# Half a step between scores and transposed scores, with the value products moved into the waits

## What is computed

```python
xn = layernorm(x)
x = x + attention0(xn) + ffn0(xn)   # key k is seen by query q where k <= q; softmax over keys
                                    # ffn0: 128 -> 512 -> gelu -> 128, inputs of both products block-quantized
xn = layernorm(x)
x = x + attention1(xn) + moe1(xn)   # causal; exp(sim - max), divided by (sum + 1e-8)
                                    # moe1: sum over 8 experts of (silu(xn @ wg) * (xn @ wu)) @ wd, 128 -> 512 -> 128
```

## Time and profile before

| what | value |
|---|---|
| median of 3 runs | 1661.28 us (1660.81 to 1663.71) |
| the profiled execution | 1662.67 us, span 1661.0 us |
| layer 0 loop, 44 to 710 us | 665.9 us; PE busy 463.6, DVE 322.4, ACT 295.9, POOL 192.1; mean clock 0.66 |
| layer 1 loop, 785 to 1640 us | 855.0 us; PE busy 819.9, DVE 658.4, ACT 507.5, POOL 448.0; mean clock 0.98 |

### The profile page before, as it was taken

One profiled execution on the slowest core, in us unless ns is written; L12 is line 12 of the kernel. 1 busy time (PEld: TensorE's weight loads), 2 busy tenths in 40 slices (PEclk: granted clock), 3 DMA queues, 4 the chain that ended last, 5 costly groups with the idle time before them and its releaser, 6 DMA issues. The chain is left out here.

```text
span 1661.0 us, 22555 instructions
## 1 busy us (share of the span) xinstructions
PE 1349.9 (81%) x7928; PEld 769.6 (46%) x7928; DVE 1032.5 (62%) x2380; ACT 827.6 (50%) x1220; POOL 681.7 (41%) x791
## 2 busy tenths in 40 slices
PE   3577767677776766644999999999999999999987
PEld 1233323333333333322556566665665656666655
DVE  5454545454545444412778787787877878878753
ACT  2444444444444443421656566565665656656650
POOL 3131324241323222332555555555555555655540
PEclk7566667676766666665999999999999999999997
DMA  5212223232222221214110111001111011000003
GB/s 155 61 53 60 60 60 98 60 98 60 81 71 72 69 86 33 67 66 114 37 28 23 47 33 44 28 24 46 34 44 28 24 46 33 25 28 24 15 14 109
DMA packets 49420, 89.67 MB, mean 54 GB/s; under 512 B 7639, under 2 KB 18396, under 8 KB 46238
## 3 DMA queue, kind: packets, MB, share of 16 engines
q1 hardware_dynamic: 48158, 87.72, 17.5%
q10 hardware_dynamic: 1152, 0.52, 0.1%
HBM read 41.69 MB, written 44.31 MB: 52 GB/s over the span
## 5 line engine op out<-in xcount | busy, mean ns | idle before, releaser
L135 PE MATMUL bank_pair<-st 24*128 24x512 f32 (+3 forms) x1024 | 234.4, 449 | 218.2 <-DVE l_mx L662 159.3
L662 DVE TENSOR_REDUCE l_mx<-bank_pair 128x2 f32<-128x1024 f32 (+1 forms) x192 | 200.4, 1045 | 320.7 <-PE bank_pair L900 320.7
L1127 POOL TENSOR_TENSOR a_h_lo<-a_h,a_h_hi 128x512 fp32r<-128x512 f32 x256 | 328.9, 1285 | 165.8 <-ACT a_h_hi L1174 164.2
L135 PEld LDWEIGHTS bank_pair<-st 24*128 24x128 f32 x1024 | 121.3, 223 | 355.9 <-issue 178.8
L1235 DVE SCALAR_TENSOR_TENSOR a_h<-a_h,bank_pair 128x512 f32<-128x512 f32 x256 | 175.4, 685 | 145.0 <-ACT a_h L1170 145.0
L749 ACT ACTIVATE l_E<-bank_pair 128x1024 f32<-128x1024 f32 (+1 forms) x192 | 168.4, 883 | 172.6 <-PE bank_pair L142 172.5
L169 DVE CUSTOM_DVE_ANT_0 bank_pair<-bank_pair,mask 128x512 f32<-128x512 f32 (+3 forms) x512 | 238.1, 517 | 8.3 <-PE bank_pair L135 8.0
L1174 ACT ACTIVATE a_h_hi<-a_h 128x512 fp32r<-128x512 f32 x256 | 161.5, 631 | 133.5 <-DVE a_h L1241 130.6
L1181 ACT ACTIVATE a_E<-bank_pair 128x1024 f32<-128x1024 f32 (+1 forms) x192 | 169.8, 884 | 115.6 <-PE bank_pair L142 115.6
L142 PE MATMUL bank_pair<-st 28*128 28x512 f32 (+3 forms) x1024 | 204.0, 438 | 1.2 <-ACT l_E L749 1.2
L1241 DVE TENSOR_TENSOR a_h<-a_h,bank 128x512 f32<-128x512 f32 x256 | 176.0, 688 | 26.7
(11 more groups left out here) (127 smaller groups left out, 2213.7 us busy)
## 6 DMA issues: line engine op xcount, KB each, us to landing
st<-stack_d SPq DMA_DIRECT2D x128, 192.0 KB
stack_d<-l_q_k_hi SPq DMA_DIRECT2D x64, 256.0 KB
stack_d<-l_q_k_lo SPq DMA_DIRECT2D x32, 256.0 KB
o_d<-l_O SPq DMA_DIRECT2D x32, 256.0 KB, 2.0
o_d<-a_O SPq DMA_DIRECT2D x32, 256.0 KB, 2.0
l_at<-o_d SPq DMA_DIRECT2D x8, 256.0 KB, 3.7
l_share<-rden_d SPq DMA_DIRECT2D x8, 256.0 KB, 3.3
a_wst<-wg_in SPq DMA_DIRECT2D x8, 256.0 KB, 2.7
```

The costliest lines, as they stand in the source:

```text
L135: return nc.tensor.matmul(bank[:, col:col + w], st[rows, j, 0, bass.ts(t, P)], st[rows, j, 1, 0:w], start=first, stop=last)
L662: nc.vector.tensor_reduce(out, src, AX.X, ALU.max).then_inc(S_used, 1)
L1127: nc.gpsimd.tensor_tensor(h_lo[:, q % RH, :], h[:, q % RH, :], h_hi[:, q % RH, :].bitcast(F32), ALU.subtract).then_inc(h_lo_ready, 1)
```

## The change

**Row groups go by heads.** The row group is now 64 r + 32 j: a quad fills all four row groups of its own `st` tile (four tiles in place of two). Its stack comes in four DMAs of 24 rows in place of two, and the maxima in two DMAs of 4 rows x 512 in place of 4 x 2 x 512; the rows that selected the plane are gone.

**Order in layer 0.** S units are cut as T units are: 512, then 384 + 128, then 256 keys, for each plane; so there are eight reductions a quad in place of six. In step g the first three positions carry T of quad g-1, units 3 to 5, and the last three T of quad g, units 0 to 2. PV of quad g-1 stands in step g behind position 4 (its first two key blocks) and behind position 5 (the other two). `turn_input(0, ..)` goes behind position 2, `project_attention` behind position 3. The order on ScalarE, POOL and DVE follows; `magic_tile` goes behind the second reduction, `store_outputs` one step later.

**Gelus.** The fc tiles are written one by one into `pv_bank` and `C_bank`, two at the end of step u == 0, one behind position 0 and one behind position 1 of u == 1; four gelus in place of two. Gelus take no bank pair any more. `keep_warm`, which nothing called, is removed.

**Layer 1.** S units are taken in the order 3, 4, 5, 0, 1, 2 (plane 1 first) so that S and T mostly lie on other row groups; `load_expert` is issued one quad later.

```diff
-def row_of(g, r):
-    return HALF * r + GROUP * (g % STACKS_A_BUFFER)
+def row_of(r, j):
+    return HALF * r + GROUP * j
 ...
-            put(("T", g, n), 0 <= g < QUADS)
+            put(("T", g - 1, n + 3) if n < 3 else ("T", g, n - 3), 0 <= (g - 1 if n < 3 else g) < QUADS)
 ...
                 scores_and_keys(g, 4)
+                if in_range(g - 1):
+                    PV(g - 1, 0)
+                    PV(g - 1, 1)
                 if q is not None:
                     turn_tile(q, min(b + 2 if u >= 2 else b + 1, B))
                 scores_and_keys(g, 5)
+                if in_range(g - 1):
+                    PV(g - 1, 2)
+                    PV(g - 1, 3)
                 if q is not None:
                     proj(q)
...
-                if in_range(g):
-                    for kb in range(NT):
-                        PV(g, kb)
 ...
-            def fc(a, half):
-                begin("F", a, half)
+            def fc(a, t):
+                if t == 0:
+                    pe.wait_ge(xqT_ready, a + 1)
+                    if a == 0:
+                        pe.wait_ge(bias_in, 16)
+                        pe.wait_ge(pv_set, 1)
+                    else:
+                        pe.wait_ge(O_copied, QUADS_A_BATCH * a)
+                elif t == 1:
+                    if a > 0:
+                        pe.wait_ge(y_added, NT * a)
+                else:
+                    pe.wait_ge(gelu_ready, NT * a + t - 1)
+                nc.tensor.matmul(h_bank(t)[:, :], xqT[:, bass.ts(t, P)], wfc[:, :], start=True, stop=False)
+                nc.tensor.matmul(h_bank(t)[:, :], onesb[:, :], bfc[:, :], start=False, stop=True).then_inc(h_ready, 1)
 ...
-                if 2 * g % B == 0 and x < EXPERTS:
+                if 2 * g % B == 2 and x < EXPERTS:
                     sp.wait_ge(w_lo_ready, 3 * x)
                     load_expert(x)
```

More of the change, by code:

```diff
@@ L128, in spread, with scores, keys_by_queries @@
     return nc.tensor.matmul(bank[:, :], sel[rows, b % 2, :], rden[rows, :], start=True, stop=True)
[L131 to L138, removed]
-    kb, col = block
[L141 to L148, removed]
+def scores(nc, bank, st, r, j, block, first, last):
+    kb, col = block
+    t, w, rows = NT - 1 - kb, width(kb), slice(row_of(r, j), row_of(r, j) + SLOT_ROWS)
+    return nc.tensor.matmul(bank[:, col:col + w], st[rows, 0, bass.ts(t, P)], st[rows, 1, 0:w], start=first, stop=last)
+def keys_by_queries(nc, bank, st, r, j, block):
+    kb, col = block
+    w, rows = width(kb), slice(row_of(r, j), row_of(r, j) + ROWS)
+    return nc.tensor.matmul(bank[:, col:col + w], st[rows, 1, bass.ts(kb, P)], st[rows, 0, N - w:N], start=True, stop=True)
 def values_by_probs(nc, pv_bank, V, E, g, kb, slots):
@@ L375, in _ @@
             load_x(1, B, x_rest_in)
[L376 to L380, removed]
+            sp.wait_ge(rows_set, 1)
+            for st in stacks:
+                for part in range(MROWS):
+                    sp.dma_start(st[SLOT_ROWS + part:P:GROUP, 1, :].bitcast(F32), st_rows[:, :]).then_inc(rows_in, 16)
             def bring_bias():
@@ L495, in rest_of_setup @@
                 nc.gpsimd.memset(mask[:, :], 0.0).then_inc(set_up, 1)
[L496 to L501, removed]
-                                            pattern=[[0, N]], channel_multiplier=-1 if plane == 0 else 1).then_inc(rows_set, 1)
+                nc.gpsimd.memset(st_rows[:, :], 1.0).then_inc(rows_set, 1)
                 pool.wait_ge(set_up, 1)
@@ L537, in _ @@
                 if in_range(g):
-                    for n in range(2, UNITS_A_QUAD):
+                    for n in range(3):
                         causal(g, n)
@@ L697, in _ @@
                     maxima_of(g + 1, 0)
-                if q is not None:
-                    magic_tile(q)
                 if u == 0 and ok(b + 1):
@@ L703, in _ @@
                     maxima_of(g + 1, 1)
+                if q is not None:
+                    magic_tile(q)
                 if u == 1 and ok(y2):
@@ L844, in _ @@
                 if in_range(g):
[L845 to L846 removed]
+                    exp(g, 1)
                 if q is not None:
@@ L857, in _ @@
                 if u == 0 and ok(b):
-                    gelus(b, 0)
-                    gelus(b, 1)
+                    for t in range(NT):
+                        gelus(b, t)
                 if g == FIRST + 3:
@@ L870, in scores_and_keys @@
             def scores_and_keys(g, n):
-                more, here = in_range(g + 1), in_range(g)
+                back, m = (g - 1, n + 3) if n < 3 else (g, n - 3)
+                more, here = in_range(g + 1), in_range(back)
                 if more:
```

207 lines of the change are left out of this document (102 added, 105 removed).

## The result

The changed kernel takes 1553.2 us at the median of four runs (1552.5 to 1553.8), against 1662.5 us for the kernel before beside it: a ratio of 0.934, 95% interval 0.932 to 0.936. The forecast was 1605 us. One execution in all the experiments, 1522.5 us of e10, ran in a slower state and is left out of that kernel's median.

A forecast was written before the change was run, and what follows sets the result against it. Layer 0 was taken as bound by a chain of waits, layer 1 by PE's own products. -44 - 11 - 6 + 5 + 0 = -56 us from 1662.67 gave 1606.7, as a median 1605 us; range 1575 to 1660.

The forecast's parts named there:

- The step's end: Layer 0, maxima to next S: S follows at once and the maxima's DMA is hidden, -4.1 us a step.
- PV in two waits: Layer 0, positions 4 and 5: PV's first part sticks out by 1.95 us, its last costs 0.78, +2.7 a step.
- The clock: Layer 0: step's end runs warm (+0.8 gained), next step's position 2 may be cold (0.5 lost), -0.3 us a step.
- Eight reductions: Layer 0, DVE: two more reductions a quad each cost the fixed part of 0.15 us, +0.3 a step.
- Fc and gelus: Two fc tiles moved into waits, -2.16 us; longer gelu chain, +1.3; net -0.8 a batch, -6 us.
- rival 4: Gelu table loads on ScalarE cost an added 1.38 us drain per switch, as the skill page says: 1627 us, chance 0.03.
- project_attention: Layer 0: moved behind position 3 it falls into a wait of 1.41 us, -11 us for 8 batches.
- Input transpose: `turn_input(0, ..)` gives up its place on the path but waits for `normalize` on DVE: nothing either way.
- Loop ends: End of layer 0's loop: the last quad's T is finished a half step later, +5 us, of 3 to 7.
- DMAs: Stack loads: four of 96 KB replace two of 192 KB, issued with PE waiting for nothing they hold; counted as 0.
- Layer 1: Shared row groups of S and T +6 us, later `load_expert` -6: zero, of -7 to +12.
- rival 3: Layer 0: all of PV runs warm, -2.8 us a step, -102 in all: 1559 us, chance 0.12.

The follow-up runs named there:

- e10: Changed kernel with three unread 128x512 matmuls behind positions 1, 2 and 3 of layer 0 steps (2 and 3 only where u == 1): 1507.1 us.
- e5: Changed kernel with T in step with S again (no half step) and four E slots instead of three: 1741.1 us.
- e12: Kernel before the change with three unread 128x512 matmuls behind positions 1, 2 and 3 of every layer 0 step: 1632.6 us.
- e2: Changed kernel with PV's first two key blocks moved behind position 5, so all of PV is one block ahead of the projection: 1605.4 us.
- e1: Changed kernel with all four PV blocks moved behind the maxima rows, at the very end of each step: 1615.2 us.
- e3: Changed kernel with all four fc tiles at the end of the step with u == 0: 1581.1 us.
- e7: Changed kernel with project_attention back at the step's end, ahead of the maxima rows, and add_attention behind the negations: 1555.9 us.
- e8: Changed kernel with normalize behind the third reduction, input transposes behind position 3, tile's magic at the previous step's end (except a batch's first tile): 1536.1 us.
- e9: Kernel before the change with one edit, layer 1's expert loads issued one quad later: 1655.9 us.
- e4: Changed kernel with layer 1's S units in natural order (plane 0 first): 1566.3 us.
- e6: Kernel before the change with each query or key store to the DRAM image in 16 groups of 8 rows instead of 8 of 16: 1652.3 us.

## Why the prediction was half right, step by step

- **The step's end, -4.1.** Right: the gap is 0.33 us. That the wait for the maxima's DMA is hidden was right too; e5 shows it at 3.0 us a step when it isn't. Missed was the second use of the half step, S and T in different rows.
- **PV in two waits, +2.7.** The parts measure 3.18 (cold) and 0.84 us, where 2.93 and 0.78 were taken. The 2.65 us that stood for a warm PV began 0.7 us ahead of the clock's rise; a PV that is warm throughout takes 2.34 us in one block (e12). In a step u == 3 the first one sticks out by 0.9 us, since `add_attention` lengthens the wait it lies in: with PV between, position 5 starts 3.07 us behind position 4's masks (327.38 to 330.45), and 2.18 us behind them in e2 (345.83 to 348.01). In another step it starts 3.65 us behind (267.27 to 270.92), so with the 1.6 us that were there without PV the first part sticks out by 2.05, where the forecast had 1.95.
- **The clock, -0.3 a step.** This step failed. The prediction set 0.8 gained at the end against 0.5 lost in the next step's position 2. In the step shown above the clock is 1.00 from the end of PV's first pair through positions 0, 1 and 2 of the next step, and over the whole loop position 2 starts warm in 16 of 31 steps, against 17 before: next to nothing was lost there. Gained are position 5 (0.54 us from its S to PV, against 0.85 in e1, where it is cold) and `proj` with the maxima rows (0.98 us from 333.47 to 334.45 in e2, against 1.87 from 357.34 to 359.21 in e1), together 1.2 us. PV itself got colder, from 4.07 to 4.32 us a quad by its four shapes. That makes -0.95 in such a step, so at most 29 us, where the sum had 9; with position 5 warm in only 20 of 31 steps it is some 26. The loops at like clock say 34.
- **Eight reductions, +0.3.** Mis-sized, by little: the reductions of layer 0 are busy for 204.6 us in 256 instead of 200.4 in 192, 0.13 us more a quad.
- **Fc and gelus, -6.** This step failed too, in its size: undoing the split costs 28 us. The tiles now run warm behind PV, 0.39 us a product instead of 0.61, so the two on the path hold S up by 1.6 us (1.93 less 0.33) where four cold ones held it by 4.32. The tiles between the positions keep position 1 warm, which the sum left out (e3). And the wait for the gelu chain, which I put at 3.9 us and so at +1.3, came in at 3.12, +0.5 over the 2.62 that the transpose had waited for `normalize` before.
- **Table load.** A load took 1.28 us and the gelu began 0.02 us behind it (349.31, 350.61). The drain that rival 4 took from the Trainium skill, "ScalarE: Activation LUTs", section "What ACT_TABLE_LOAD costs", is not seen here either.
- **project_attention, -11.** Worth 3 (e7): behind position 3 it waits for POOL's division and runs cold, 3.16 us in all, and behind PV it would have been warm.
- **Input transpose, "nothing either way".** Wrong by its consequence: `turn_input(0, ..)` behind position 2 waits up to 3.5 us a batch for `normalize`, which the change left behind the moved `magic_tile` on DVE. u == 2 gained only 1.1 us, and e8 took 3.1 more out of it.
- **Loop ends, +5.** From the last marker of layer 0 to the last copy of PV's output it is 23.5 us instead of 17.5, so +6.0: right. What turned the sign was behind it: the stores of the next point (7.3 of the 11 us) and warm products of the batch before the last (queries 1.13 us instead of 2.07); how the rest divides stays open.
- **DMAs, 0.** Wrong by -10: the sum looked at the loads and not at the stores, whose image's layout the change also alters. Only where nothing covers them does it count, at the start and between the layers.
- **Layer 1, 0.** The -6 measured -8 (e9). The +6 is some +4 by e4, and about as much came back from a cause that no run isolates.

The nearest number of the prediction, rival 3 with 1559 us, was right by accident. It wanted all of PV warm. PV's largest form takes 1041 ns in the mean after, against 965 before (140 to 560 us): PV got colder, and what surrounds it got warm.

The sum missed 53 us: fc tiles 15 to 22 (e3), the clock around PV some 20, stores 10 (e6), layer 1 8 (e9), and `project_attention` -8 (e7), together 45 to 52. So two terms of the sum carry most of the miss, the clock and the fc tiles, and one that stood at nothing, the stores. Of these the clock's part alone is worked out from rows and not from a run that changes nothing else; the runs give it a size (34 less 9) but can't part it from the warm fc tiles.

## What to carry to other kernels

When products are moved in a kernel that isn't bound by TensorE, price each of them at both clock levels, list which neighbours change level with it, and check the sum against one run in which idle gaps are filled with unread products. A transfer whose bytes and destination stay the same can still change its speed by the shape of its access pattern: compare the DMA share of such a transfer, not only its size. When a tensor's layout and the phase between two streams change together, ask what each does without the other, for here the new layout without the half step costs 188 us.

## What was not expected of the hardware

Stores of 256 KB with 8 groups in their slowest dimension ran at a DMA share of 0.50 and 177 GB/s, with 16 groups at 0.94 to 0.96 and 314 to 316 GB/s; the edit in the kernel before gave 10 us. The Trainium skill, "DMA: Bandwidth & Descriptors", section "Why a DMA increments its semaphore by 16 and not by 1", says that the number of engines a DMA uses is the largest one up to 16 that divides the slowest dimension of both its patterns. The rows agree, and I had not weighed it.

Unread products in the waits of layer 0 raised its clock from 0.73 to 0.84 and took 46 us off (3%), though nine more products stand in most steps. In the kernel before the same products gave only 29 us and a clock of 0.76: its steps still hold a wait for the maxima's DMA (13.7 us in 12 records from 140 to 560 us, 2.6 at most), and PV began warm in 5 of 30 steps, against 24 of 30 in the kernel after with fillers.
